# Layer 1's first expert product: three chunks of 512, 512 and 160 + 160 columns in place of four of 336

## The reference

```
for e in range(E):
    h = x @ W1[e] + b1[e]             # 256 -> 1344
    a, g = jnp.split(h, 2, axis=-1)   # 672 values, 672 gates
    act = a * jax.nn.silu(g)
    out = out + cw[:, e:e + 1] * (act @ W2[e] + b2[e])
```

## Time and profile before

| | |
|---|---|
| median of three runs | 560.01 us |
| the three runs | 560.01, 557.59, 751.81 us |
| the profiled execution's own time | 557.76 us |
| its span, first to last instruction | 556.0 us |
| mean granted TensorE clock | 0.995 |
| busy: PE, PEld, DVE, ACT, POOL | 526.5, 467.9, 329.5, 339.9, 248.5 us |
| layer 1's experts | about 359 to 544 us of the span |

### The profile page before, as it was taken

How to read it: one execution, slowest core, us unless ns; L and a number is a source line. 1 busy time by engine, 2 the same in 40 slices (tenths; PEclk the granted TensorE clock), 3 DMA queues, 4 the chain that set the end, 5 groups by cost and what they waited for, 6 DMA issues and landing times.

```text
span 556.0 us, 15295 instructions
## 1 busy us (share of the span) xinstructions
PE 526.5 (95%) x3516; PEld 467.9 (84%) x3517; DVE 329.5 (59%) x770; ACT 339.9 (61%) x657; POOL 248.5 (45%) x278
## 2 busy tenths in 40 slices
PE   7999979999999999999999999799999999999995
PEld 3887638889999899999878876499999999999894
DVE  5647873555533555555575478745766666767542
ACT  5786625666655666666647856255677676767450
POOL 5659022343644355554354270224545364545432
PEclk9999999999999999999999999899999999999999
DMA  7645745876432454224550428463374656321211
GB/s 256 199 135 151 257 132 164 267 177 164 113 77 39 147 111 96 36 44 124 163 170 7 152 79 284 148 214 93 64 201 111 176 129 161 82 38 29 40 24 20
DMA packets 49037, 70.54 MB, mean 127 GB/s; under 512 B 9182, under 2 KB 40560, under 8 KB 49008
## 3 DMA queue, kind: packets, MB, share of 16 engines
q1 hardware_dynamic: 35216, 56.41, 32.3%
q0 software_dynamic: 10464, 13.58, 13.6%
q10 hardware_dynamic: 3328, 0.20, 0.4%
HBM read 57.55 MB, written 13.47 MB: 128 GB/s over the span
## 4 chain that ended last, share of the span: by engine, by line
PE 75%; DMA 6%; issue 5%; DVE 5%; ACT 3%; DVEq 3%; ACTq 1%; POOL 1%; POOLq 0%; SPq 0%
PE banks L1351 15%; PE banks L1353 15%; PE banks L1352 15%; PE banks L1576 5%; PE banks L1413 5%; PE banks L1501 4%; PE banks L1359 3%; PE banks L1477 3%; DMA expert_io<-xn_dram,gcol 2%; PE banks L1541 2%; PE banks L1631 2%; DMA mid_dram<-region_b,scol 1%; DVEq L1229 1%; PE banks L1424 1%; DMA xres<-in_x_dram 1%
## 5 line engine op out<-in xcount | busy, mean ns | idle before, releaser
L1351 PE MATMUL banks<-w_hi,xT_hi 128*128 x336 | 119.3, 355 | 4.3 <-DVE xT_lo L1220 2.6
L1353 PE MATMUL banks<-w_hi,xT_lo 128*128 x336 | 114.9, 342 | 0.0
L1352 PE MATMUL banks<-w_lo,xT_hi 128*128 x336 | 114.2, 340 | 0.0
L1351 PE MATMUL banks<-w_hi,hT_hi 128*128 x364 | 107.9, 296 | 3.7 <-DVE hT_lo L1298 2.7
L1353 PE MATMUL banks<-w_hi,hT_lo 128*128 x364 | 102.8, 283 | 0.0
L1352 PE MATMUL banks<-w_lo,hT_hi 128*128 x364 | 102.8, 282 | 0.0
L842 ACT COPY banks<-seed_rows 128x672 f32 (+1 forms) x84 | 69.0, 822 | 25.8 <-DVE h_sb L1315 10.3
L652 POOL DMA_INDIRECT mid_dram<-region_b,scol x26 | 49.6, 1909 | 77.3 <-DMA mid_dram<-region_b,scol 28.7
L625 POOL TENSOR_TENSOR w_lo<-raw,w_hi 128x1024 fp32r<-128x1024 f32 (+2 forms) x24 | 58.8, 2467 | 46.3 <-ACT w_hi L697 39.3
L652 POOL DMA_INDIRECT out_dram<-region_b,scol x26 | 46.1, 1772 | 72.2 <-DMA expert_io<-xn_dram,gcol 22.0
L1351 PEld LDWEIGHTS banks<-w_hi,hT_hi 128*128 128x128 f32 x364 | 69.3, 190 | 6.9 <-issue 6.0
(11 more groups left out here) (211 smaller groups left out, 872.0 us busy)
## 6 DMA issues: line engine op xcount, KB each, us to landing
raw<-in_L_ffn_w_dram SPq DMA_DIRECT2D x32, 512.0 KB, 3.8
raw<-in_L_ffn_W_dram SPq DMA_DIRECT2D x16, 672.0 KB, 3.9
seed_rows<-in_L_ffn_b_dram SPq DMA_DIRECT2D x8, 672.0 KB
seed_rows<-in_L_ffn_b_dram SPq DMA_DIRECT2D x8, 512.0 KB
xn_dram<-raw SPq DMA_DIRECT2D x6, 512.0 KB, 3.1
raw<-in_L_ffn_W_dram SPq DMA_DIRECT2D x8, 384.0 KB, 3.4
raw<-in_L_ffn_W_dram SPq DMA_DIRECT2D x8, 256.0 KB
wqkv<-in_L_conv_W_qkv_dram SPq DMA_DIRECT2D x2, 768.0 KB, 5.6
```

What stands on the lines that cost most here:

```text
L1351: pe.matmul(out, hi, w_high, start=first, stop=False, skip_group_check=onto)
L1352: pe.matmul(out, hi, w_low, start=False, stop=False, skip_group_check=onto)
L1353: return pe.matmul(out, lo, w_high, start=False, stop=last, skip_group_check=onto)
```

## The change

The first product of layer 1 is cut into three chunks: the first 512 gates (into bank 1), the first 512 values (bank 0), and the last 160 values with the last 160 gates as one product of 320 columns read in two runs (bank 2). PE does them in this order. The seeds become one of 1024 columns (banks 0 and 1) and one of 320 (bank 2); in ACT's step the wide one now stands ahead of `xT_hi` and the narrow one behind it. The SiLUs take 512 and 160 columns; the second waits for the third chunk. h is made in parts of 512 and 160, the first after the second chunk, the second after the third. The wide seed waits for the first part of h, the narrow one for the second. The h transpose's two groups become 4 and 2 tiles. Layer 0 keeps its two chunks of 512.

```diff
--- before.py
+++ after.py
@@ -59,15 +59,16 @@
 
 
 class Ffn:
-    def __init__(self, wide, full, tail, first_tiles, chunk):
-        self.wide, self.full, self.tail, self.chunk, self.chunks = wide, full, tail, chunk, wide // chunk
+    def __init__(self, wide, full, tail, first_tiles, chunk, chunks):
+        self.wide, self.full, self.tail, self.chunk, self.chunks = wide, full, tail, chunk, chunks
         self.kt = full + int(tail > 0)
         self.hidden = full * P + tail
         self.tiles = (slice(0, first_tiles), slice(first_tiles, self.kt))
         self.seed_wide = wide + (0 if tail else C)
 
 
-FFN = [Ffn(wide=1024, full=8, tail=0, first_tiles=4, chunk=512), Ffn(wide=1344, full=5, tail=32, first_tiles=2, chunk=336)]
+FFN = [Ffn(wide=1024, full=8, tail=0, first_tiles=4, chunk=512, chunks=2),
+       Ffn(wide=1344, full=5, tail=32, first_tiles=4, chunk=512, chunks=3)]
 
 
 STACK_LOW, STACK_BIAS_LOW, STACK_ROWS = 64, 96, 98
@@ -229,7 +230,7 @@
         v_logits = sb("v_logits", [BN, PIX, E])
         lg2 = sb("lg2", [P, TILES, E])
         prob8 = sb("prob8", [P, TILES, E])
-        past_io = expert_io[:, 2 * C + FFN[1].chunk * 2:]
+        past_io = expert_io[:, 2 * C + FFN[1].hidden:]
         cand = past_io[:, 0:TILES * E].rearrange("p (i e) -> p i e", i=TILES)
         m_top = sb("m_top", [P, TOPK, TILES])
         pick = sb("pick", [P, TOPK, TILES, E], BF16)
@@ -261,7 +262,7 @@
 
         xg = expert_io[:, 0:2 * C]
         y_rows = region_b[:, KC * TOKENS - PAIRS * P // 2:KC * TOKENS - PAIRS * P // 2 + 2 * C]
-        silu_g = expert_io[:, 2 * C:2 * C + FFN[1].chunk * 2]
+        silu_g = expert_io[:, 2 * C:2 * C + FFN[1].hidden]
         last_hots = [raw[:, 1, n * TILES * P:(n + 1) * TILES * P].rearrange("p (i t) -> p i t", i=TILES) for n in range(2)]
         last_y = [raw[:, 1, (2 * TILES + 2 * n) * P:][:, 0:C] for n in range(2)]
         last_rel = sb("last_rel", [P, 2, TILES])
@@ -820,7 +821,7 @@
 
                 act.wait_ge(s.tab, 2)
                 if f.tail:
-                    nc.scalar.copy(bank[5][STACK_BIAS_LOW:P, 3 * P:4 * P], one_rows[STACK_BIAS_LOW:P, :]
+                    nc.scalar.copy(bank[5][STACK_BIAS_LOW:P, P:2 * P], one_rows[STACK_BIAS_LOW:P, :]
                                    ).then_inc(s.bias_hot, 1)
 
                 def xT_high(b):
@@ -833,14 +834,18 @@
                 def expert_of(b):
                     return act.value_load(col(tab_e, b), min_val=0, max_val=E - 1)
 
-                def seed(b, e, pair):
-
-                    chunks = slice(2 * pair, 2 * pair + 2)
+                def seed(b, e, part):
+
                     act.wait_ge(seed_in, e + (E * L + 1))
                     if after(b, 1):
-                        act.wait_ge((s.h, s.silu)[pair] if L else s.h, 2 * b)
-                    nc.scalar.copy(banks[:, chunks, 0:f.chunk], seed_row(L, e % SEED_ROWS)[:, 0:f.wide]
-                                   .rearrange("p (c n) -> p c n", c=f.chunks)[:, chunks, :]).then_inc(s.seeded, 1)
+                        act.wait_ge(s.h, 2 * b - (1 - part) if L else 2 * b)
+                    row = seed_row(L, e % SEED_ROWS)[:, 0:f.wide].rearrange("p (v n) -> p v n", v=2)
+                    if part == 0:
+                        copy = nc.scalar.copy(banks[:, 0:2, :], row[:, :, 0:f.chunk])
+                    else:
+                        copy = nc.scalar.copy(bank[2][:, 0:2 * (f.hidden - f.chunk)].rearrange("p (v n) -> p v n", v=2),
+                                              row[:, :, f.chunk:f.hidden])
+                    copy.then_inc(s.seeded, 1)
 
                 def split(q, b):
 
@@ -869,7 +874,7 @@
                         if L == 0 and j == 1 and ahead:
                             e_next = expert_of(b + 1)
                             pieces = piece_range(act, b)
-                        act.wait_ge(s.h_mm, f.chunks * b + j + 1)
+                        act.wait_ge(s.h_mm, f.chunks * b + (j + 1, 2 * j + 1)[L])
                         if L == 0:
                             if after(b, 1):
                                 act.wait_ge(s.hT_mm, 2 * b)
@@ -878,24 +883,25 @@
                         else:
                             if after(b, 1):
                                 act.wait_ge(s.h, 2 * b)
-                            nc.scalar.activation(silu_g[:, f.chunk * j:f.chunk * (j + 1)], bank[2 + j][:, 0:f.chunk],
+                            gates = (bank[1][:, :], bank[2][:, f.hidden - f.chunk:2 * (f.hidden - f.chunk)])[j]
+                            nc.scalar.activation(silu_g[:, f.chunk * j:min(f.chunk * (j + 1), f.hidden)], gates,
                                                  ACT.Silu).then_inc(s.silu, 1)
                             if ahead and j == 0:
                                 e_next = expert_of(b + 1)
                     if not ahead:
                         return
                     if L == 1:
-                        seed(b + 1, e_next, 1)
+                        seed(b + 1, e_next, 0)
                         pieces = piece_range(act, b)
                     xT_high(b + 1)
-                    seed(b + 1, e_next, 0)
+                    seed(b + 1, e_next, L)
                     if after(b, 2):
                         for_pieces(act, pieces, lambda q: split(q, b))
 
                 act.wait_ge(swept, 4 * (L + 1))
                 e_first = expert_of(0)
-                for pair in range(L, -1, -1):
-                    seed(0, e_first, pair)
+                for part in range(L + 1):
+                    seed(0, e_first, part)
                 xT_high(0)
                 block_loop(act, step, 1, s.tab)
                 if L == 0:
@@ -1292,7 +1298,7 @@
                             part = f.tiles[j]
                             if f.tail and j == 1:
                                 rows = slice(f.tail, 2 * f.tail)
-                                nc.vector.tensor_tensor(hT_hi[rows, f.full, :], bank[5][rows, 3 * P:4 * P],
+                                nc.vector.tensor_tensor(hT_hi[rows, f.full, :], bank[5][rows, P:2 * P],
                                                         hT_hi[rows, f.full, :].bitcast(F32), ALU.subtract)
                                 part = slice(part.start, f.full)
                             nc.vector.tensor_tensor(hT_lo[:, part, :], bank[4 + j][:, 0:(part.stop - part.start) * P]
@@ -1304,17 +1310,18 @@
                     if L == 1 and not last:
                         for j in range(2):
                             dve.wait_ge(s.silu, 2 * b + j + 1)
-                            dve.wait_ge(s.h_mm, f.chunks * b + 3 + j)
+                            dve.wait_ge(s.h_mm, f.chunks * b + 2 + j)
                             if j == 1:
                                 again = STACK_BIAS_LOW // f.tail - 1
                                 nc.vector.tensor_tensor(
                                     h_sb[:, f.hidden:f.hidden + again * f.tail].rearrange("p (r n) -> p r n", r=again),
-                                    bank[1][:, f.chunk - f.tail:f.chunk].unsqueeze(1).to_broadcast([P, again, f.tail]),
+                                    bank[2][:, f.hidden - f.chunk - f.tail:f.hidden - f.chunk].unsqueeze(1)
+                                    .to_broadcast([P, again, f.tail]),
                                     silu_g[:, f.hidden - f.tail:f.hidden].unsqueeze(1).to_broadcast([P, again, f.tail]),
                                     ALU.mult)
-                            nc.vector.tensor_tensor(h_sb[:, f.chunk * j:f.chunk * (j + 1)], bank[j][:, 0:f.chunk],
-                                                    silu_g[:, f.chunk * j:f.chunk * (j + 1)], ALU.mult
-                                                    ).then_inc(s.h, 1)
+                            part = slice(f.chunk * j, min(f.chunk * (j + 1), f.hidden))
+                            nc.vector.tensor_tensor(h_sb[:, part], bank[2 * j][:, 0:part.stop - part.start],
+                                                    silu_g[:, part], ALU.mult).then_inc(s.h, 1)
                             if ahead and after(b, 2):
                                 pieces = (pieces_before(dve, b - 1),) if j == 0 else (pieces[0], pieces_before(dve, b))
                     if ahead:
@@ -1541,7 +1548,18 @@
                         mm = pe.transpose(bank[7][:, k * P:(k + 1) * P], rows[:, k * P:(k + 1) * P], ident[:, :])
                     mm.then_inc(s.xT_mm, 1)
 
-                order = (0, 1) if L == 0 else (2, 3, 0, 1)
+                def chunk_of(w, c):
+                    if L == 0:
+                        return w[:, c * f.chunk:(c + 1) * f.chunk]
+                    values_gates = w.rearrange("p (v n) -> p v n", v=2)
+                    return values_gates[:, c, 0:f.chunk] if c < 2 else values_gates[:, :, f.chunk:f.hidden]
+
+                def chunk_out(c):
+                    if L == 0 or c < 2:
+                        return bank[c][:, :]
```

(8 more changed lines are left out.)

## The result

The kernel after takes 580.38 us (median of four runs, 579.57 to 580.73) against 559.78 for the kernel before in the same comparison: a ratio of 1.0387, with a 95% interval of 1.0347 to 1.0427. The ratio is taken over fast runs alone and leaves out a run of 751.81 us of the kernel before, so it is not the quotient of these medians. The kernel is slower by 3.9%, and 6 us above the upper end of the range (559 to 574). The profiled execution took 580.04 us, with a span of 578.3, at a mean granted clock of 0.998.

A forecast was written before the change was run, and what follows sets the result against it. PE bounded the kernel before; after the change PE would wait for ACT's later xT_hi. The profiled 557.76 us, plus 9.4 over 25 steps, less 0.2 for products 0, 1 and 27, gave 567; range 559 to 574.

The forecast's parts named there:

- Where pieces are split: Layer 1 steps with pieces: with one, h ends 0.3 us before the seed, step 6.85; with two, step 8.15 us.
- the sum: Layer 1's 25 steps: 21 x 6.85 + 4 x 8.15 = 176.45 us against 167.03 before, +9.4.
- Rival B: DVE sets the step too: L1333 0.5 us later delays h, 0.35 per one-piece step; kernel 573 us; chance 0.15.
- Part 2: ACT and DVE, same work reordered: xT_hi behind wide seed and table reads; PE waits 0.45 us, step 6.85 for 6.48.
- Rival A: ACT's table reads cost nothing: next product at 6.41 us into the step, kernel 556 us; chance 0.12.
- Part 1: PE, layer 1's first product: 18 matmuls for 24, same columns, saving 0.08 us a block, 2.2 us over 28 blocks.
- rival C: PE's two-run tail product streams no faster than 512 columns: 0.48 us later in each of 25 steps, 579; chance 0.03.

The follow-up runs named there:

- gates_tail_values: Kernel after with its three chunks reordered to gates, tail, values, a seed for each, ACT's split ahead of the last seed: 554.04 us, 0.9925 of the kernel before.
- before_split_early: Kernel before with ACT's split ahead of its second seed in layer 1: 558.89 us, 0.9987 of the kernel before.
- reads_early: Kernel after with ACT's two table reads moved between the SiLUs in layer 1: 565.93 us, 1.0146 of the kernel before.
- acts_old_order: Kernel after with ACT's table reads between the SiLUs and xT_hi ahead of the wide seed: 561.32 us, 1.0043 of the kernel before.

## Why the prediction was wrong

- **The step that failed** is "Where pieces are split": "One piece: h from 3.25 to 3.93, 0.3 before the seed: just hidden." Measured in the step above, h runs from 403.25 - 399.06 = 4.19 to 4.87, and the seed waits for it. The prediction carried the 2.43 from L1333 to hT_lo in the earlier trace rows over as DVE's own time. Most of it is: where the split waits for nobody, in gates_tail_values, the same distance is 399.02 - 396.67 = 2.35. But the idle time in front of the split, 0.49, also holds 0.08 of a wait for ACT's piece, and this is the part that grows: in the kernel after the distance is 402.02 - 398.57 = 3.45. The prediction moved xT_hi by a whole microsecond on ACT and didn't ask what stands behind it there: the split, for which DVE waits. This costs 10.1 us in steps with one piece and 3.9 in those with two, 14.0 of the 14.9 by which the 25 steps exceed the sum; the other 0.9 are three of the nine steps without pieces, and why these are late is open.
- The circle was there to be read before. In one step of the kernel before, ACT's piece ends at 397.16 + 1.17 = 398.33 and DVE's split starts 0.73 later, as after (the view calls it "issue"); h follows, the second seed waits for it, and ACT's piece stands right behind. ACT's timeline:

```profile
397.16 1.17 ACT L850 CAST w_hi<-raw  x2
...
402.98 0.72 ACT L842 COPY banks<-seed_rows 128x672 f32 x1 [0.24 <-DVE h_sb L1315]
403.64 1.17 ACT L850 CAST w_hi<-raw  x2
```

and DVE's split in that step:

```profile
399.06 1.19 DVE L1229 TENSOR_TENSOR w_lo<-raw,w_hi  x1 [0.49 <-issue]
```

It closed in 403.64 - 397.16 = 6.48, PE's own step, and before_split_early shows that PE sets that step. From seed to piece took 0.66; after the change it takes 1.40 + 0.27 + 0.57 = 2.24, or 1.58 more. From the start of h to the seed it takes 0.86 for 402.98 - 401.75 = 1.23, or 0.37 less, since the wide seed waits for the first part of h alone: 6.48 + 1.58 - 0.37 = 7.69.
- **Rival B** named the right symptom, h as releaser of the seed, with a chance of 0.15, but the wrong mechanism (L1333 late behind an output scatter) and half the price: 0.35 a step, where 0.84 were measured. What it gave for itself, that DVE's rows have no gap there, is not so: DVE stands idle for 0.49 ahead of the split in both steps of the earlier trace rows, at 424.98 and 431.46.
- **Part 2** was right: the chain from the last matmul over the seed and the reads to the next product is met within 0.05 in quiet steps, and reads_early shows that the reads are its 0.42. **Rival A** is out with it.
- **Part 1** was right in kind, off in size. Chunks of 320 columns take (402.81 - 401.93)/6 = 0.147 a matmul, as taken, so **rival C** is out. Those of 512 take (401.93 - 399.39)/11 = 0.231 against the 0.227 of the earlier trace rows, and the product's first matmul 0.33 instead of 0.313. So a block saves some 0.03, not 0.08; where PE fills the steps they are 6.44 in acts_old_order and 6.47 in gates_tail_values, against 6.48.
- Outside the steps the profiled runs differ by -2.0: 580.04 - 557.76 = 22.3 is 24.3 in the 25 steps less 1.7 by which the first product starts earlier (357.52 against 359.19) and 0.4 at both ends.

## What to carry to other kernels

When an instruction moves later on an in-order engine, follow what stands behind it on that engine to whoever waits for that, and go on until the path ends or comes back: two engines that wait for each other once per step make a circle, and its length, not either engine's busy share, is the least that a step can take. A distance between two rows is not a duration; before it is carried to another kernel as a cost, the idle time in it has to be taken out and given to whoever ends it, even if it is small. And the same chunks in another order (gates, tail, values) take 554 us for 580: there only the seed that the next product needs last waits for the last thing that this one makes.

## What the runs showed of the hardware that was not expected

- A split piece costs DVE's instruction stream at least 1.25 to 1.27 us: there are 0.45 of work in 64-word pieces and 1.41 in full ones, and hT_lo starts that much, or 1.46, after the split. Likewise 0.72 to 0.74 pass between the end of ACT's piece and the start of DVE's split, which waits for it, in every kernel here where it waits; the split's address arithmetic runs in that time (DVEq L1235, from 399.87 in the step above).
- Matmuls of 512 columns come 0.231 apart in layer 1's first product and mostly 0.227 in layer 0's, at the same granted clock of 1.00. Why stays open; no run was made for it.
- Time moves outside the changed code: the first product of layer 1 starts between 356.3 and 364.8 us in the ten profiles, ahead of every step that was changed. The three latest starts (361.3, 364.6 and 364.8) are those of the three lowest mean granted clocks (0.988, 0.987 and 0.983; the others 0.995 and more), so the clock goes with at least part of it. Steps, read within one profile, told more here than whole runs did.
